# Input tiles scaled by ScalarE in the first layer, and VectorE's late weights in pieces over more steps

## The chip, the cores and the metric

The kernel runs on one core of a Trainium2 chip. The metric is the device time of one execution in microseconds; for the kernel before, the median of three runs is 833.73 (832.03 to 834.83). Engines are named TensorE (PE in the rows), VectorE (DVE), ScalarE (ACT), GpSimd (POOL) and SyncE (SP).

## The reference

The input x is 8 sequences of 512 rows by 128 columns. Four blocks follow, each as `x = x + layernorm(block(layernorm(x)))`:

```
block 1: 6 layers of   x = softmax(q) @ (softmax(k)^T v) @ wo + bo + x      (8 heads, on layernorm(x))
                       x = leaky_relu(layernorm(x) @ w1) @ w2 + x
block 2: squared relu of x @ W_fc^T, @ W_proj^T, then 5 steps of a spiking unit, counted
block 3: x @ Win^T + bin; k = sum_n C*dB*exp(logdA*t); a convolution by rfft/irfft of length 1024;
         + u * Dp; @ Wout^T + bout
block 4: token shift, sigmoid gate and squared relu key, value
```

The first `layernorm(x)` of block 1 is what part one of the change computes elsewhere: `(x - m) / sqrt(v + eps)` for each sequence. The spectrum of k, which depends on weights alone, is what part two spreads out.

## The kernel before, in words

**Layout.** X holds the whole input (8 x 512 columns), XI the running stream. A sequence is 4 tiles of 128x128. An item is one sequence in one layer: 48 items, item n is sequence b = n % 8 of layer n // 8. Every engine has a function `step(n, b, layer)` that lists, in the order in which this engine executes them, operations of item n and of earlier items (`run(f, n - 2)` is f for item n-2). `layers(step)` unrolls steps 0 to 43; what follows is an order written out by hand. Engines wait for each other by counting semaphores alone, so a step of one engine may be early or late against another's.

**One item.** ScalarE makes XR (L929), XI times a root RSTD that GpSimd computed. TensorE turns it (L317; its start is the beginning of a step on TensorE), ScalarE copies it out twice (XTH, XTF, L934), VectorE takes the difference XTL (L1363). TensorE makes keys and queries. VectorE takes the keys' maximum NKM (L1379), ScalarE the exponential EK (`keys_exp`, L976) and the copy QF, VectorE turns QF into QB (L1389) and takes the maximum QMX (L1395), GpSimd subtracts it (`queries_shift`, L772), ScalarE takes the exponential (L998), VectorE sums (L1399) and inverts (L1405), GpSimd multiplies (`queries_scale`, L777), VectorE turns it to QS (L1356). ScalarE's XR of the next item (L929) stands behind the queries' exponential. Two steps later the second half of the item: X2H and X2F from ScalarE, X2L from VectorE (`second_low`, L1329), then four hidden blocks on TensorE (X2H, X2L with W1) and their products with W2.

**The first layer's input.** For each sequence VectorE computes mean and variance (`input_stats`, L1264 and L1267, to STX and MVX), GpSimd the root of the variance (`input_rstd`, L721 to L727, to RX and VNX), and then XI = (X - mean) * RX. For sequence 0 this last is VectorE's, for the other seven it is GpSimd's `input_norm` (L731): four tiles of 128x128 with two columns of scalars each. It stands at the end of GpSimd's step n for sequence n+3, ahead of `join(n + 1)`, which joins the statistics of the stream (JOIN, L743 to L749), `first_root` (RSTD, L767) and `queries_shift`.

**The weights of later blocks.** In steps 31 to 41 the spectrum of block 3's kernel is made beside the layers. CENTRE is step 33, CENTRE_IN step 34. VectorE's `late_weights(n)` adds Dp to KTM in step 33, makes sums and differences of KTM in steps 34 to 36 (`butterfly_pairs`, `butterfly_even`, `butterfly_odd`, to FLY and KV), and in step 34 also NMU and the centred WOUTT and BOUT (L1425 to L1429). It stands in VectorE's step between `first_stats` and `second_low`:

```
                run(first_stats, n + 2)
...
                late_weights(n)
...
                run(second_low, n - 2)
                run(masked, n)
```

KTM is complete at the end of step 32 (`k_out`), KV is needed in step 37 (`ktm`), the centred weights by the last blocks (`mixed`). `part_done` makes an engine wait for its own instruction before it goes on. `keep_busy` on TensorE multiplies CE1 into a bank that is not used yet, to fill steps 0 to 2.

## Time and profile before

| | before |
|---|---|
| median of 3 runs | 833.73 us (832.03 to 834.83) |
| the profiled execution, its own time | 833.7 us |
| its span | 831.3 us |
| TensorE busy | 771.9 us, 93% |
| VectorE busy | 663.1 us, 80% |
| ScalarE busy | 579.2 us, 70% |
| GpSimd busy | 442.4 us, 53% |

The profile describes one execution. The span runs from the first to the last instruction; the execution's own time is 2.4 us longer. A busy share is an average over the whole span, so it doesn't say which engine sets the pace of a stretch. For that one reads what ended an engine's idle time (in square brackets behind an instruction), and the granted clock of TensorE.

### The profile page before, as it was taken

The numbers are of one execution on the slowest core, as the hardware profiler recorded it, in microseconds if no ns is written. First come the engines' busy times: TensorE is split into PE (matmuls) and PEld (weight loads), VectorE is DVE, ScalarE is ACT, GpSimd is POOL, SyncE is SP. The second block draws the span as 40 slices with busy tenths as digits, with TensorE's granted clock in tenths as the row PEclk, the third lists the DMA queues.
The fourth block names the chain that finished last, engine by engine and source line by source line (L and its number), as shares of the span: only waits on it lengthen the run. The fifth ranks groups of instructions, "written<-read, shape, count | busy, mean of one in ns | idle before, by whom it ended". The sixth has DMA issues, their size and how long they took to land.

```text
span 831.3 us, 16083 instructions
## 1 busy us (share of the span) xinstructions
PE 771.9 (93%) x5266; PEld 674.8 (81%) x5274; DVE 663.1 (80%) x1957; ACT 579.2 (70%) x1252; POOL 442.4 (53%) x724
## 2 busy tenths in 40 slices
PE   7689999999999999999999999999999999997672
PEld 3478889999999999999988898988878977885651
DVE  4667888788777887778787777788868999999873
ACT  3476777787777777777875777768885586755464
POOL 6888455555466544544452443644554244555454
PEclk9999999999999999999999999999999999999988
DMA  9300000100010000100001000000000000000001
GB/s 252 106 1 1 1 1 2 39 2 1 1 39 2 1 2 1 40 2 1 1 2 39 1 1 1 2 1 1 2 1 1 2 0 2 2 13 0 27 13 52
DMA packets 19728, 13.69 MB, mean 16 GB/s; under 512 B 2488, under 2 KB 18495, under 8 KB 19647
## 3 DMA queue, kind: packets, MB, share of 16 engines
q1 hardware_dynamic: 19646, 12.67, 5.4%
q8 instruction: 43, 0.70, 0.4%
q14 instruction: 39, 0.31, 0.1%
HBM read 10.57 MB, written 2.10 MB: 15 GB/s over the span
## 4 chain that ended last, share of the span: by engine, by line
PE 72%; DVE 13%; POOL 8%; issue 4%; ACT 2%; DMA 0%; POOLq 0%; DVEq 0%; ACTq 0%
PE PS L307 65%; PE PS L317 7%; POOL XI L731 3%; DVE ST L1196 2%; POOL RX L722 1%; DVE MV L1199 1%; POOL QB L772 1%; DVE BIG L1503 1%; POOL RSTD L767 1%; ACT XI L886 1%; POOL R L689 1%; DVE STX L1264 0%; DVE BIG L1552 0%; DVE BIG L1496 0%; DVE BIG L1497 0%
## 5 line engine op out<-in xcount | busy, mean ns | idle before, releaser
L307 PE MATMUL PS<-W,HL 128*128 128x128 f32 x1536 | 202.6, 275 | 0.0
L307 PEld LDWEIGHTS PS<-W,HL 128*128 128x128 f32 x1536 | 194.1, 192 | 9.8 <-issue 1.4
L942 ACT ACTIVATE HL<-PS 128x512 f32<-128x512 f32 x192 | 109.9, 596 | 17.7 <-PE PS L307 13.9
L743 POOL TENSOR_TENSOR JOIN<-STATS 128x8 f32<-128x8 f32 (+1 forms) x48 | 12.0, 249 | 184.5 <-DVE STATS L1279 184.5
L307 PE MATMUL PS<-X2H,W1L 128*128 128x512 f32 x192 | 89.1, 464 | 3.3 <-issue 3.0
L976 ACT ACTIVATE EK<-PS,NKM 128x512 f32<-128x512 f32 x48 | 33.1, 689 | 75.4 <-DVE NKM L1379 75.4
L777 POOL TENSOR_TENSOR QB<-QB,QRC 128x512 f32<-128x512 f32 x48 | 50.9, 1060 | 55.7 <-DVE QRC L1405 55.7
L307 PE MATMUL PS<-X2H,W1H 128*128 128x512 f32 x192 | 76.4, 398 | 0.0
L307 PE MATMUL PS<-X2L,W1H 128*128 128x512 f32 x192 | 76.1, 396 | 0.0
L1279 DVE BATCH_NORM_STATS2 STATS<-XI 128x6 f32<-128x128 f32 x352 | 75.5, 278 | 0.1
L317 PE MATMUL PS<-ID,XR 128*128 128x128 f32 x384 | 59.0, 276 | 8.6 <-ACT XR L929 8.6
L934 ACT ACTIVATE XTH<-PS,LNC,SC 128x512 fp32r<-128x512 f32 x48 | 37.4, 779 | 42.1 <-PE PS L317 42.1
L689 POOL TENSOR_TENSOR R<-VE,MHALF 128x4 f32<-128x4 f32 x56 | 61.0, 1089 | 4.7
L929 ACT ACTIVATE XR<-XI,RSTD 128x128 f32<-128x128 f32 x192 | 61.0, 394 | 3.4 <-POOL RSTD L767 3.4
L688 POOL TENSOR_SCALAR VE<-MV 128x4 f32<-128x4 f32 x56 | 13.4, 240 | 90.6 <-DVE MV L1199 88.4
L760 POOL TENSOR_TENSOR RSTD<-JOIN,MHALF 128x4 f32<-128x4 f32 x48 | 61.0, 1271 | 0.2
L317 PEld LDWEIGHTS PS<-ID,XR 128*128 128x128 f32 x384 | 46.4, 146 | 15.0 <-issue 12.1
L307 PE MATMUL PS<-MM,QS 128*128 128x128 f32 x384 | 53.7, 284 | 1.8 <-DVE QS L1356 1.8
L307 PE MATMUL PS<-EKT,XR 128*128 128x128 f32 x384 | 51.0, 276 | 1.6 <-ACT EKT L881 1.6
L772 POOL TENSOR_TENSOR QB<-QB,QMX 128x512 f32<-128x512 f32 x48 | 51.9, 1081 | 0.2 <-DVE QMX L1395 0.2
L1389 DVE STREAM_TRANSPOSE QB<-QF 128x512 f32<-128x512 f32 x48 | 34.1, 711 | 22.4 <-ACT QF L881 21.9
L307 PEld LDWEIGHTS PS<-MM,QS 128*128 128x128 f32 x384 | 47.5, 195 | 4.4 <-issue 4.3
(217 smaller groups left out, 2091.9 us busy)
## 6 DMA issues: line engine op xcount, KB each, us to landing
W<-in_w SPq DMA_DIRECT2D x12, 256.0 KB
X<-in_x SPq DMA_DIRECT2D x8, 256.0 KB, 4.6
out<-X SPq DMA_DIRECT2D x8, 256.0 KB, 2.3
QKV<-in_qkv SPq DMA_DIRECT2D x6, 192.0 KB, 2.7
FWD<-in_fwd SPq DMA_DIRECT2D x1, 1024.0 KB, 5.4
INV<-in_inv SPq DMA_DIRECT2D x1, 1024.0 KB, 8.1
WO<-in_wo SPq DMA_DIRECT2D x6, 64.0 KB
FWDX<-in_fwdx SPq DMA_DIRECT2D x1, 256.0 KB, 5.7
```

The lines of the kernel that those rows point to most:

```text
L307: return nc.tensor.matmul(o, l, r, start=start, stop=stop, skip_group_check=True)
L317: last = nc.tensor.transpose(o[:, j * P:(j + 1) * P], i[:, j * P:(j + 1) * P], ID[:, :])
L689: return pool.tensor_tensor(RS[k][:, :], VES[k][:, :], MHALF[:, 0:TILES], ALU.pow)
L760: pool.tensor_tensor(RSTD[:, TILES:2 * TILES], JOIN[:, 4, TILES:2 * TILES], MHALF[:, TILES:2 * TILES], ALU.pow).then_inc(s["ln2_rstd"], 1)
L772: pool.tensor_tensor(heads(QB[:, :]), heads(QB[:, :]), QMX[:, :].unsqueeze(2).broadcast_to([P, 32, DH]), ALU.subtract).then_inc(s["q_sub"], 1)
L777: pool.tensor_tensor(heads(QB[:, :]), heads(QB[:, :]), QRC[:, :].unsqueeze(2).broadcast_to([P, 32, DH]), ALU.mult).then_inc(s["q_nrm"], 1)
L929: last = nc.scalar.activation(o[:, j * P:(j + 1) * P], tile(src, b, j), ACT.Copy, scale=r[:, first + j:first + j + 1])
L934: return nc.scalar.activation(o[:, :], i[:, :], ACT.Identity, scale=SC[slot][:, which:which + 1], bias=LNC[slot][:, 2 * which + 1:2 * whic ...
L942: nc.scalar.activation(HL[f][:, :], pH[f % 2][:, :], ACT.Prelu, alpha=LEAK).then_inc(s["hl"], 1)
L976: nc.scalar.activation(EK[:, :], pK[:, :], ACT.Exp, bias=NKM[:, 0:1], accum_out=KSM[:, 0:1]).then_inc(s["ek"], 1)
L1279: last = nc.vector.bn_stats(STATS[:, first + j, :], tile(src, b, j))
L1389: nc.vector.transpose(QB[:, :], QF[:, :]).then_inc(s["q_blk"], 1)
```

## The change

Part one: GpSimd's `input_norm` becomes `input_mean`, which computes -mean * RX for the four tiles in two 128x4 operations, to NMX. ScalarE gets `input_norm`: XI = X * RX + NMX, one activation with scale and bias columns per tile (`normalise`, L886 before). It stands ahead of `keys_exp` in steps 0 (sequence 1) and 1 to 5 (sequences 3 to 7), and behind `weights_copy` in step 0 (sequence 2). VectorE's `input_stats(n + 3)` moves from the end of the step to the place behind `first_stats`. Sequence 0 stays on VectorE.

Part two: of `late_weights`, NMU and WOUTT go to step 27 (MIXED = 3 * 8 + 3), BOUT to step 28, both behind `second_stats`. The butterfly is split: `band_sums` behind `second_stats`, ahead of the queries' blocks, and `band_differences` behind `second_low`, each in the same steps as before.

```diff
+MIXED = 3 * BATCH + 3
...
-            def input_norm(b):
-                for j in range(b * TILES, (b + 1) * TILES):
-                    last = pool.tensor_scalar(XI[:, j * P:(j + 1) * P], X[:, j * P:(j + 1) * P], MVX[:, 2 * j:2 * j + 1],
-                                              RX[:, j:j + 1], ALU.subtract, ALU.mult)
-                last.then_inc(s["xi_init"], 1)
+            def input_mean(b):
+
+                cols = slice(b * TILES, (b + 1) * TILES)
+                mean = MVX[:, b * 2 * TILES:(b + 1) * 2 * TILES].rearrange("p (j t) -> p j t", t=2)[:, :, 0]
+                part_done(pool.tensor_tensor(NMX[:, cols], mean, RX[:, cols], ALU.mult))
+                pool.tensor_scalar(NMX[:, cols], NMX[:, cols], -1.0, 0.0, ALU.mult, ALU.add).then_inc(s["i_nm"], 1)
...
                     input_rstd(n + 3)
-                    input_norm(n + 3)
+                    input_mean(n + 3)
...
+            def input_norm(b):
+                act.wait_ge(s["i_nm"], b)
+                tiled = slice(b * TILES, (b + 1) * TILES)
+                normalise(seq(XI, b), seq(X, b), RX[:, tiled], NMX[:, tiled]).then_inc(s["xi_init"], 1)
...
                 run(rectified, n - 3, 2)
+                if n == 0:
+                    input_norm(1)
+                if 1 <= n < BATCH - 2:
+                    input_norm(n + 2)
                 run(keys_exp, n)
...
                 run(weights_copy, n)
+                if n == 0:
+                    input_norm(2)
...
+            def band_sums(n):
+                if n == CENTRE:
+                    dve.wait_ge(s["k_out"], 2)
+                    part_done(tt(KTM[0:1, 0:P], KTM[0:1, 0:P], DP[0:1, :], ALU.add))
+                if n == CENTRE + 1:
+                    tt(FLY[:, 0:2 * P], KTM[:, 0:2 * P], KTM[:, 2 * P:4 * P], ALU.add)
+                if n == CENTRE + 2:
+                    ts(FLY[:, 4 * P:6 * P].rearrange("p (i c) -> p i c", c=P),
+                       FLY[:, 0:4 * P].rearrange("p (i h c) -> p i h c", i=2, h=2)[:, :, 1], 0.5 ** 0.5, None, ALU.mult)
+                    tt(KV[:, 0:P], FLY[:, 0:P], FLY[:, P:2 * P], ALU.add)
+                if n == CENTRE + 3:
+                    tt(tile(KV, 0, 2), KTM[:, 0:P], FLY[:, 5 * P:6 * P], ALU.add)
+                    tt(tile(KV, 0, 3), FLY[:, 4 * P:5 * P], KTM[:, 2 * P:3 * P], ALU.add)
...
+            def band_differences(n):
+                if n == CENTRE + 1:
+                    part_done(tt(FLY[:, 2 * P:4 * P], KTM[:, 0:2 * P], KTM[:, 2 * P:4 * P], ALU.subtract))
+                if n == CENTRE + 2:
+                    tt(KV[:, P:2 * P], FLY[:, 0:P], FLY[:, P:2 * P], ALU.subtract)
+                    part_done(nc.vector.tensor_copy(KV[:, 4 * P:6 * P], FLY[:, 2 * P:4 * P]))
+                if n == CENTRE + 3:
+                    tt(tile(KV, 0, 6), KTM[:, 0:P], FLY[:, 5 * P:6 * P], ALU.subtract)
+                    tt(tile(KV, 0, 7), FLY[:, 4 * P:5 * P], KTM[:, 2 * P:3 * P], ALU.subtract).then_inc(s["ktm"], 1)
...
                 run(second_stats, n - 1)
+                late_weights(n)
+                band_sums(n)
...
                 run(first_stats, n + 2)
+                if n + 3 < BATCH:
+                    input_stats(n + 3)
...
-                late_weights(n)
...
                 run(second_low, n - 2)
+                band_differences(n)
                 run(masked, n)
                 run(queries_sum, n)
                 run(queries_reciprocal, n)
                 run(second_residual, n - 3)
-                if n + 3 < BATCH:
-                    input_stats(n + 3)
```

How the orders stand. ScalarE from the second copy of the turned stream to the exponential of the keys in step 3, before and then in the change (HL are hidden blocks, EK the keys' exponential):

```order
L934 ACTIVATE XTF<-PS,LNC,SC 128x512
L942 ACTIVATE HL<-PS 128x512 x2
L976 ACTIVATE EK,KSM<-PS,NKM 128x512
L881 ACTIVATE QF<-PS 128x512
L942 ACTIVATE HL<-PS 128x512
```

```order
L936 ACTIVATE XTF<-PS,LNC,SC 128x512
L949 ACTIVATE HL<-PS 128x512 x2
L888 ACTIVATE XI<-X,NMX,RX 128x128 x4
L983 ACTIVATE EK,KSM<-PS,NKM 128x512
L883 ACTIVATE QF<-PS 128x512
L949 ACTIVATE HL<-PS 128x512
```

Four tiles of XI now stand directly ahead of EK.

VectorE in step 2, from the queries' maximum to the end of the step, before and then in the change:

```order
L1395 TENSOR_REDUCE QMX<-QB 128x32
L1383 RECIPROCAL KRC<-KSM 128x1
L1329 TENSOR_TENSOR X2L<-X2F,X2H 128x512
L1411 TENSOR_TENSOR CT<-PS,HMASK 128x128
L1399 TENSOR_REDUCE QSM<-QB 128x32
L1405 RECIPROCAL QRC<-QSM 128x32
L1264 BN_STATS STX<-X 128x6 x4
L1267 BN_AGGR MVX<-STX 128x2 x4
```

```order
L1408 TENSOR_REDUCE QMX<-QB 128x32
L1396 RECIPROCAL KRC<-KSM 128x1
L1277 BN_STATS STX<-X 128x6 x4
L1280 BN_AGGR MVX<-STX 128x2 x4
L1342 TENSOR_TENSOR X2L<-X2F,X2H 128x512
L1424 TENSOR_TENSOR CT<-PS,HMASK 128x128
L1412 TENSOR_REDUCE QSM<-QB 128x32
L1418 RECIPROCAL QRC<-QSM 128x32
```

The statistics of X have moved ahead of X2L.

VectorE in step 34, from the stream's statistics to the mask, before and then in the change:

```order
L1279 BN_STATS STATS<-XI 128x6 x4
L1292 TENSOR_TENSOR FLY<-KTM 128x256
L1293 TENSOR_TENSOR FLY<-KTM 128x256
L1425 TENSOR_SCALAR NMU<-MU 128x2
L1427 BN_STATS WST<-WOUTT 128x6
L1428 BN_AGGR WMV<-WST 128x2
L1429 TENSOR_SCALAR WOUTT<-WOUTT,WMV 128x128
L1427 BN_STATS WST<-BOUT 128x6
L1428 BN_AGGR WMV<-WST 128x2
L1429 TENSOR_SCALAR BOUT<-BOUT,WMV 128x128
L1329 TENSOR_TENSOR X2L<-X2F,X2H 128x512
L1411 TENSOR_TENSOR CT<-PS,HMASK 128x128
```

```order
L1292 BN_STATS STATS<-XI 128x6 x4
L1431 TENSOR_TENSOR FLY<-KTM 128x256
L1402 STREAM_TRANSPOSE QB<-QF 128x512
L1408 TENSOR_REDUCE QMX<-QB 128x32
L1396 RECIPROCAL KRC<-KSM 128x1
L1292 BN_STATS STATS<-XI 128x6 x4
L1342 TENSOR_TENSOR X2L<-X2F,X2H 128x512
L1442 TENSOR_TENSOR FLY<-KTM 128x256
L1424 TENSOR_TENSOR CT<-PS,HMASK 128x128
```

X2L follows the statistics at once, one FLY stands ahead of QB and one behind X2L. TensorE's and SyncE's orders are the same in both kernels.

## Rows read from the trace of the kernel before

**Rows 1.** The page, part 1: busy time, share of the span, instructions of each engine.

```profile
PE 771.9 (93%) x5266; PEld 674.8 (81%) x5274; DVE 663.1 (80%) x1957; ACT 579.2 (70%) x1252; POOL 442.4 (53%) x724
```

**Rows 2.** The chain of waits over 0 to 120 us, shares by line.

```profile
by line: PE PS L307 23.4%; POOL XI L731 18.5%; POOL RX L722 6.8%; POOL QB L772 6.0%; issue 5.5%; POOL RSTD L767 5.1%; PE PS L317 3.4%; DVE STX L1264 3.3%; POOL VNX L725 2.7%; DMA X<-in_x 2.3%; DVE QSM L1399 1.7%; POOL QB L777 1.7%; ACT QB L
```

**Rows 3.** Stretches from turn to turn: length; busy of PE, PEld, DVE, ACT, POOL; clock, DMA, GB/s.

```profile
24.37:36.33 11.96, 8.46 (x37) 5.53 (x37) 8.17 (x25) 5.40 (x13) 11.12 (x19) 0.86 0.25 72
36.33:48.61 12.28, 8.88 (x46) 6.02 (x47) 8.87 (x26) 6.78 (x15) 11.36 (x21) 1.00 0.01 2
...
61.30:74.32 13.02, 12.02 (x82) 10.43 (x83) 9.38 (x27) 8.78 (x19) 10.71 (x19) 1.00 0.00 0
74.32:87.33 13.01, 12.02 (x82) 10.43 (x83) 9.99 (x31) 8.78 (x19) 10.69 (x19) 1.00 0.01 2
526.92:538.43 11.51, 11.51 (x83) 10.40 (x82) 9.02 (x23) 8.67 (x18) 6.54 (x11) 1.00 0.00 1
```

**Rows 4.** Timeline of step 4: start, duration, engine, line, operation [idle before it <- what ended it].

```profile
61.17 1.06 POOL L777 TENSOR_TENSOR QB<-QB,QRC 128x512 f32<-128x512 f32 x1 [0.88 <-DVE QRC L1405]
...
62.92 0.20 POOL L721 TENSOR_SCALAR VEX<-MVX 128x4 f32<-128x4 f32 x1 [0.69 <-DVE MVX L1267]
...
65.58 3.13 POOL L731 TENSOR_SCALAR XI<-X,MVX,RX 128x128 f32<-128x128 f32 x4
...
66.70 0.69 ACT L976 ACTIVATE EK<-PS,NKM 128x512 f32<-128x512 f32 x1 [2.32 <-DVE NKM L1379]
...
68.95 0.69 DVE L1395 TENSOR_REDUCE QMX<-QB 128x32 f32<-128x512 f32 x1
...
70.73 0.69 DVE L1329 TENSOR_TENSOR X2L<-X2F,X2H 128x512 fp32r<-128x512 f32 x1 [1.02 <-ACT X2F L934]
...
70.95 1.39 POOL L772 TENSOR_TENSOR QB<-QB,QMX 128x512 f32<-128x512 f32 x1
...
74.58 0.86 DVE L1264 BATCH_NORM_STATS2 STX<-X 128x6 f32<-128x128 f32 x4
...
75.47 0.38 DVE L1267 BATCH_NORM_AGGREGATE MVX<-STX 128x2 f32<-128x6 f32 x4
```

**Rows 5.** Timeline of step 0's end: the mask, its matmul, and the turn of step 1.

```profile
18.40 0.27 DVE L1233 TENSOR_SCALAR MBV<-HMASK,BIAS 128x128 f32<-128x128 f32 x1
...
19.29 0.38 PE L307 MATMUL PS<-WO,MBV 128*128 128x128 f32 x2
...
24.37 0.63 PE L317 MATMUL PS<-ID,XR 128*128 128x128 f32 x4 [2.92 <-ACT XR L929]
```

**Rows 6.** Timeline of step 34.

```profile
431.04 0.71 DVE L1389 STREAM_TRANSPOSE QB<-QF 128x512 f32<-128x512 f32 x1 [0.75 <-ACT QF L881]
...
432.92 0.78 ACT L934 ACTIVATE X2F<-PS,LNC,SC 128x512 f32<-128x512 f32 x1
...
433.65 1.18 POOL L760 TENSOR_TENSOR RSTD<-JOIN,MHALF 128x4 f32<-128x4 f32 x1
433.89 0.41 DVE L1293 TENSOR_TENSOR FLY<-KTM 128x256 f32<-128x256 f32 x1
...
436.14 0.68 DVE L1329 TENSOR_TENSOR X2L<-X2F,X2H 128x512 fp32r<-128x512 f32 x1
...
436.92 0.47 PE L307 MATMUL PS<-X2H,W1L 128*128 128x512 f32 x1 [1.85 <-issue]
```

**Rows 7.** Stretches of steps 34, 35 and 36, columns as in rows 3.

```profile
424.82:439.12 14.30, 12.45 (x85) 11.11 (x84) 12.20 (x33) 9.07 (x19) 7.38 (x12) 0.96 0.01 2
439.12:452.16 13.04, 12.62 (x84) 11.41 (x83) 9.95 (x26) 8.78 (x18) 4.57 (x10) 0.91 0.23 61
452.16:464.11 11.95, 11.65 (x83) 10.56 (x82) 10.06 (x27) 8.79 (x18) 5.09 (x10) 1.00 0.01 2
```

**Rows 8.** ScalarE's timeline: the same form of activation on X, in a later block.

```profile
683.89 1.64 ACT L886 ACTIVATE XI<-X,NM,R 128x128 f32<-128x128 f32 x4
```

**Rows 9.** Waits of the whole span: engine and line, what it waited for, us, times, longest.

```profile
DVE CT L1411 <- PE PS L307: 31.8, 41, 2.0
```

More of the change, by code:

```diff
@@ L183, in build @@
         STX, MVX = sb("STX", [BATCH * TILES * 6]), sb("MVX", [BATCH * TILES * 2])
-        VEX, RX, VNX = (sb(n, [BATCH * TILES]) for n in ("VEX", "RX", "VNX"))
+        VEX, RX, VNX, NMX = (sb(n, [BATCH * TILES]) for n in ("VEX", "RX", "VNX", "NMX"))
         XR2 = sb("XR2", [SEQ])
@@ L226, in build @@
             "bias_out bias_ps bm_out bm_ps bo_c c_in c_ps ce1 ce1_zero ct e1 e1_arg e2 e2_arg eighth ek ekT_ps "
-            "ek_tm fc_out fc_ps g_ps gt h_ps hl i_rstd i_var k_fm k_out k_ps k_rec kf kf_ps kmax ktm la la_exp "
+            "ek_tm fc_out fc_ps g_ps gt h_ps hl i_nm i_rstd i_var k_fm k_out k_ps k_rec kf kf_ps kmax ktm la la_exp "
             "late_in ln1_rstd ln2_rstd ln_part m_ps m_ready mbv mixed out_ps p_part q0_in q_blk q_exp q_fm "
@@ L854, in _ @@
             input_rstd(1)
-            input_norm(1)
+            input_mean(1)
             input_rstd(2)
-            input_norm(2)
+            input_mean(2)
             layers(step)
@@ L1411, in masked @@
                 tt(CT[:, :], pK[:, P:2 * P], HMASK[:, :], ALU.mult).then_inc(s["ct"], 1)
-            def late_weights(n):
+            def band_sums(n):
                 if n == CENTRE:
@@ L1417, in late_weights @@
                 if n == CENTRE + 1:
-                    butterfly_pairs(KTM)
+                    tt(FLY[:, 0:2 * P], KTM[:, 0:2 * P], KTM[:, 2 * P:4 * P], ALU.add)
                 if n == CENTRE + 2:
-                    butterfly_even(KV)
+                    ts(FLY[:, 4 * P:6 * P].rearrange("p (i c) -> p i c", c=P),
+                       FLY[:, 0:4 * P].rearrange("p (i h c) -> p i h c", i=2, h=2)[:, :, 1], 0.5 ** 0.5, None, ALU.mult)
+                    tt(KV[:, 0:P], FLY[:, 0:P], FLY[:, P:2 * P], ALU.add)
                 if n == CENTRE + 3:
-                    butterfly_odd(KTM, KV).then_inc(s["ktm"], 1)
-                if n == CENTRE_IN:
+                    tt(tile(KV, 0, 2), KTM[:, 0:P], FLY[:, 5 * P:6 * P], ALU.add)
[9 more added lines that the diff above has]
+                    tt(tile(KV, 0, 7), FLY[:, 4 * P:5 * P], KTM[:, 2 * P:3 * P], ALU.subtract).then_inc(s["ktm"], 1)
+            def late_weights(n):
+                if n == MIXED:
                     dve.wait_ge(s["late_in"], LATE_LOADS)
                     ts(NMU[:, :], MU[:, :], -1.0, 1.0, ALU.mult, ALU.add)
-                    for t in (WOUTT, BOUT):
-                        part_done(nc.vector.bn_stats(WST[:, :], t[:, :]))
+                for at, weights in ((MIXED, WOUTT), (MIXED + 1, BOUT)):
+                    if n == at:
+                        part_done(nc.vector.bn_stats(WST[:, :], weights[:, :]))
                         part_done(nc.vector.bn_aggr(WMV[:, :], WST[:, :]))
-                        last = ts(t[:, :], t[:, :], WMV[:, 0:1], None, ALU.subtract)
+                        last = ts(weights[:, :], weights[:, :], WMV[:, 0:1], None, ALU.subtract)
+                if n == MIXED + 1:
                     last.then_inc(s["mixed"], 1)
```

## The prediction

> **What bounds the kernel now.** The page comes first: TensorE is busy 93% of the span [rows 1], the others 53 to 80%, so a gain must be time in which TensorE waits or runs below full speed. There are two such places that the change touches. I call the start of a step on TensorE its turn (the first transpose of XR); step n works on item n.
>
> First place, steps 0 to 6. The chain of waits over the first 120 us names GpSimd's input tiles (L731) for 18.5%, more than any other line but the matmuls [rows 2]. The table of stretches, cut at the turns 24.37, 36.33, 48.61, 61.30, 74.32 and 87.33, shows what that does [rows 3]: steps 4 and 5 take 13.02 and 13.01 us for 82 matmul records, while a step of the same work late in the stack (83 records, TensorE never idle) takes 11.51. So 11.51 is the floor of a full step; steps 3 to 5 (12.69, 13.02, 13.01) stand 4.2 us above it together. Steps 1 and 2 hold only 37 and 46 records and run at the latency of one item's chain. In step 4 this chain can be read [rows 4]: GpSimd scales the queries (to 62.23), computes the next sequence's rstd, writes its tiles for 3.13 us, joins the statistics, and so reaches the queries' shift (L772) at 70.95, though the maximum it needs was there at 69.64. Step 0 ends with 2.92 us in which TensorE waits for XR [rows 5].
>
> Second place, steps 34 to 36. VectorE's spectrum pieces and the last weights stand ahead of X2L. X2F is ready at 433.70, X2L starts at 436.14, TensorE stands still for 1.85 us and goes on at 436.92 [rows 6]. Behind that the granted clock falls from 2.4 to 1.2 GHz for a while: it is 0.96 and 0.91 of full speed on average over steps 34 and 35 [rows 7].
>
> Between them and from there to the last layers TensorE is full, and the order of every engine is fixed, so what is won in either place moves everything behind it by the same amount.
>
> **The change, part 1: the input tiles.** GpSimd loses 7 times 3.13 us and gets two 128x4 operations instead, each as VEX's 0.20 [rows 4], 0.55 us with their issue: it is freed of 7 x 2.58, about 18 us, all in the first 85. ScalarE gets 7 times four activations that read a scale and a bias column from memory. The nearest row is the same form on X much later: four take 1.64 us [rows 8]. VectorE keeps its work, but input_stats, 0.86 + 0.38 = 1.27 us with the gap [rows 4], moves from the end of a step to the place ahead of X2L, and in step 0 ahead of the mask that TensorE's output bias waits for. Step by step, until the turns agree with the floor:
>
> - Step 0. With the tiles on ScalarE (in its waits for the keys' maximum and the transposed weights) XR is ready at about 21 by the same durations, and TensorE comes to the turn when its own merge is done, 24.37 - 2.92 = 21.45. The moved statistics push the mask by 1.27; it was ready at 18.67 and used at 19.29, so of the 0.62 of slack I count 0.42 as usable. The turn comes at about 22.3: gain 2.92 - 0.85 = 2.1 [rows 5].
> - Steps 1 and 2. The new tiles of item n+2 stand ahead of keys_exp on ScalarE, wait there for GpSimd's mean, and take 1.64. By step 4 (below) the exponential comes 0.5 us late; here the keys are not held up by other matmuls, so I estimate 1. Everything of the item is queued behind it, and in step 2 the moved statistics (1.27) also stand ahead of X2L. Against this stand GpSimd's lateness at the shift, 70.95 - 69.64 = 1.3 in step 4, and the slow clock of step 1 (0.86 on average [rows 3]), which I expect gone with the 2.92 us wait ahead of it. I take step 1 as 0.15 and step 2 as 0.6 slower, an estimate: turns at 34.4 and 47.3, gain 1.3 so far.
> - Steps 3 and 4. The mean is ready 0.93 (end of L777) + 3.35 - 0.69 (the chain to the tiles, less the idle before it, for which the moved statistics come earlier) + 0.55 = 4.2 us after the turn; the tiles end at 5.8, the exponential starts at 5.9 instead of 5.40. The maximum of the queries is 0.5 later, the statistics' 1.27 follow, and X2L starts at 10.1 instead of 9.43. This is 0.7 over the floor: 12.2 instead of 12.69 and 13.02, gain 0.5 and 0.8.
> - Step 5 has no statistics left; the shift follows the maximum at once (8.9 instead of 9.65), XR is ready before TensorE is, and the step costs 11.7 instead of 13.01: gain 1.3. Step 6 has no tile in either kernel and its own VectorE work (decay): unchanged.
>
> Sum of part 1: 1.3 + 0.5 + 0.8 + 1.3 = 3.9 us. The bounds: at best steps 3 to 5 sit on the floor and step 0 gains its whole 2.92, together 7.1; at worst the steps gain nothing and steps 1 and 2 each lose a whole 1.64 against step 0's 2.1, that is -1.2. What hides the tiles is ScalarE's idle time before the exponential, 2.32 us in step 4; without it each group would cost its 1.64.
>
> **Part 2: the spectrum.** In step 34 nine VectorE instructions leave the place ahead of X2L. One FLY addition goes behind second_stats, into a wait of 0.75 us for QF [rows 6], one subtraction behind X2L, where VectorE waits for TensorE ahead of CT (31.8 us in 41 waits [rows 9]), and the rest to steps 27 and 28 into the same wait. X2L then starts with X2F, at 433.7, over a microsecond before TensorE asks for it. What returns, with step 36 as the measure (11.95 us, TensorE busy 11.65 of them [rows 7]): in step 34 the idle 1.85 and, for the slow clock, 12.45 - 11.65 - 0.25 for one matmul more = 0.55; in step 35 the idle 13.04 - 12.62 = 0.42 and the slow clock's 12.62 - 11.65 = 0.97; in step 36 the idle 0.30, ahead of which the same pieces stand. Together 4.1. The bounds are 0 and 4.1 plus a few tenths. The seven other instructions took 436.14 - 434.30 = 1.84, so steps 27 and 28 get some 0.9 each in a wait of 0.75 and may come 0.3 late; step 33's KTM addition shares its wait with W2M and may make the queries 0.4 late. I cost these at 0, because X2L still waits for X2F behind them; without that cover they cost 0.3 + 0.3 + 0.4 = 1.0. No DMA moves, and no order on TensorE or SyncE.
>
> One row and one rule differ. The FLY subtraction, with two inputs in SBUF, ran from 433.89 to 434.30 inside GpSimd's pow of 433.65 to 434.83 [rows 6]; nothing blocked it. By the Trainium skill, "SBUF — State Buffer", section "SBUF: two separate sides", a VectorE instruction with two SBUF inputs and a GpSimd instruction share a port pair as an exclusive lock, and the later one waits for the whole of the earlier one. By that rule the pieces behind X2L in steps 34 to 36 would wait for GpSimd's pow, 3 x 0.4 us, and the time would be 826.9; the trace speaks against it here, for a pow of 4 columns at least.
>
> **Sum.** 3.9 + 4.1 = 8.0 less. The profiled execution took 833.7 (span 831.3), the median of the three runs is 833.73, so both give 825.7.
>
> **The rivals.**
> - A, full first layer: the late exponential is absorbed, since the keys are not what TensorE wants next, and part 1 gives step 0's 2.1 and the 4.2 to the floor, 6.3. For it: ScalarE had 2.32 us of idle there. Against it: X2L stands behind QMX and the moved statistics. 833.7 - 10.4 = 823.3.
> - B, poor first layer: the tiles ahead of the exponential take back what GpSimd gives, or the clock falls once more in the thin steps 1 to 3 (TensorE is busy 8.5 to 8.9 of their 12 us [rows 3]). With 1.5 lost in steps 1 and 2 each and 1.6 gained in steps 3 to 5, part 1 gives 2.1 - 3.0 + 1.6 = 0.7: 828.9.
> - C, part 2 stays short: something else is late for X2L in step 34, or the pieces behind X2L wait for GpSimd's pow. TensorE idles 1 us and the clock may fall again: part 2 gives 1 to 2.8: 828.8 to 827.0. The row of the free overlap and X2F at 433.70 speak against it.
> - D, slower: the tiles on ScalarE become the bound of steps 1 to 5. Each step is longer by 1.64, 8.2 in all, and TensorE's longer waits let the clock fall twice at the 1.5 that it cost in steps 34 and 35: 8.2 + 3.0 - 2.1 - 4.1 = 5.0 slower, 838.7. It decides from the point at which GpSimd's mean comes later than the keys' maximum plus the slack of the shift (0.85 us); I have it 0.5 too late.
> - The change doing something else than it says: the listing of the orders excludes that.
>
> **How the numbers follow.** Forecast 0.60, A 0.17, B 0.12, C 0.06, D 0.03, and 0.02 for both parts weak at once. Predicted: 825.7. The range 822.5 to 829.5 takes in A with a microsecond to spare, and B and C. A measurement of this kernel can tell about 0.3%, 2.5 us: faster means below 831.2. All but D and the doubly weak case and a slice of B lie there: faster 0.93, same 0.04, slower 0.03.
>
> **What would show it.** In the profile after: no granted clock below 1.00 from 430 to 450, no idle on TensorE ahead of X2H,W1L in steps 34 to 36 and X2L following X2F at once; turns at about 22, 34, 47, 59.5, 71.8 and 83.5; the four tiles on ScalarE at 1.64 us, directly ahead of the exponential, which starts 5.8 to 6 us after the turn. The step that I trust least is the price of that order in steps 1 to 4. If the exponential starts as early as before, A is right; if steps 3 and 4 stay at 13, B. If a clock of 0.5 remains near step 34, my reading of part 2 is wrong.

## The result, and the profile after

The median of four runs went from 833.45 us to 823.40 (822.92 to 823.64); the ratio is 0.9868, 95% interval 0.9841 to 0.9894. That is 10.05 us less, where 8.0 had been forecast. Measured once more later, beside the experiments, the change had a median of 825.49 over five runs against 833.83 (ratio 0.9899, 0.9874 to 0.9924), 8.3 less. Both medians lie in the forecast range; the forecast 825.7 is 2.3 above the first and 0.2 above the second. Why the change itself moves between 822.9 and 827.7 is a question of its own below. One of the six executions of part 1 alone took 1119.06 us at a mean clock of 0.651; its median below is that of the other five.

The profiled execution took 823.64 us with a span of 821.6, against 833.7 and 831.3. Busy times are those of the page, part 1; the columns are as in [rows 1].

```profile
PE 768.5 (94%) x5274; PEld 672.3 (82%) x5274; DVE 661.7 (81%) x1957; ACT 588.0 (72%) x1280; POOL 424.8 (52%) x710
```

GpSimd has 17.6 us less, ScalarE 8.8 more. The chain of waits over the first 120 us, by line, answers to [rows 2]:

```profile
by line: PE PS L308 39.9%; PE PS L318 7.5%; ACT XI L888 6.7%; POOL RX L723 5.1%; issue 4.8%; POOL QB L779 4.4%; ACT EK L983 3.6%; DMA X<-in_x 2.4%; POOL VNX L726 2.3%; DVE QSM L1412 2.0%; DVE STX L1277 1.4%; DVE QRC L1418 1.2%; DVE QB L1402
```

GpSimd's tiles are gone from it, ScalarE's have 6.7% in place of 18.5%, and the matmuls' share has risen from 23.4 to 39.9%. The stretches from turn to turn, steps 0 to 5, columns as in [rows 3]:

```profile
9.89:22.04 12.15, 8.40 (x39) 5.31 (x40) 6.78 (x29) 9.20 (x23) 6.41 (x15) 1.00 1.04 305
22.04:33.88 11.84, 6.98 (x39) 4.51 (x37) 8.79 (x27) 6.91 (x16) 8.23 (x17) 1.00 0.48 137
33.88:46.84 12.96, 9.84 (x46) 7.25 (x47) 8.79 (x25) 8.73 (x19) 9.25 (x20) 0.87 0.01 2
46.84:58.76 11.92, 11.71 (x84) 10.45 (x83) 8.80 (x25) 9.99 (x22) 7.53 (x17) 1.00 0.00 0
58.76:70.70 11.94, 11.73 (x83) 10.44 (x82) 9.27 (x27) 9.99 (x22) 7.55 (x17) 1.00 0.01 1
70.70:82.61 11.91, 11.70 (x84) 10.33 (x83) 8.95 (x23) 9.96 (x22) 7.97 (x17) 1.00 0.01 2
```

Steps 3 to 5 now take 11.9 us, 0.4 over the floor (11.51); step 0 is 2.5 shorter (the turn before it was at 9.72, now at 9.89); step 2 is longer than before and at 0.87 of full clock. Step 4 in the timeline, which answers to [rows 4]:

```profile
59.77 0.19 POOL L722 TENSOR_SCALAR VEX<-MVX 128x4 f32<-128x4 f32 x1
...
62.82 1.65 ACT L888 ACTIVATE XI<-X,NMX,RX 128x128 f32<-128x128 f32 x4 [1.00 <-POOL NMX L735]
...
64.38 0.67 ACT L983 ACTIVATE EK<-PS,NKM 128x512 f32<-128x512 f32 x1
...
65.04 0.58 ACT L883 ACTIVATE QF<-PS 128x512 f32<-128x512 f32 x1
...
65.19 0.66 PE L318 MATMUL PS<-ID,EK 128*128 128x128 f32 x4 [0.21 <-ACT EK L983]
...
66.39 0.69 DVE L1408 TENSOR_REDUCE QMX<-QB 128x32 f32<-128x512 f32 x1
...
67.06 0.85 DVE L1277 BATCH_NORM_STATS2 STX<-X 128x6 f32<-128x128 f32 x4
67.16 1.06 POOL L774 TENSOR_TENSOR QB<-QB,QMX 128x512 f32<-128x512 f32 x1 [0.62 <-DVE QMX L1408]
...
68.25 0.66 DVE L1342 TENSOR_TENSOR X2L<-X2F,X2H 128x512 fp32r<-128x512 f32 x1
```

Counted from the turn at 58.76, the exponential starts at 5.62 (before: 5.40), because the keys' maximum is there at 4.65 (before: 5.37) and the tiles hold it up by 0.97. QF starts at 6.28 (6.27), QMX at 7.63 (7.65), GpSimd's shift at 8.40 (9.65) and X2L at 9.49 (9.43). The exponential is 0.2 late and TensorE waits 0.21 for it; nothing behind it is late. X2F is ready at 9.16 and X2L starts 0.33 behind it, where the statistics end.

Step 34, which answers to [rows 6]:

```profile
428.39 0.78 ACT L936 ACTIVATE X2F<-PS,LNC,SC 128x512 f32<-128x512 f32 x1
...
429.20 0.69 DVE L1342 TENSOR_TENSOR X2L<-X2F,X2H 128x512 fp32r<-128x512 f32 x1 [0.42 <-ACT X2F L936]
429.21 1.54 POOL L762 TENSOR_TENSOR RSTD<-JOIN,MHALF 128x4 f32<-128x4 f32 x1
429.81 0.42 DVE L1442 TENSOR_TENSOR FLY<-KTM 128x256 f32<-128x256 f32 x1
```

X2L starts 0.03 us behind X2F's end, and TensorE has no idle time there. The stretches of steps 34, 35 and 36, against [rows 7]:

```profile
420.28:432.08 11.80, 11.80 (x86) 10.68 (x85) 9.67 (x25) 8.94 (x19) 6.82 (x12) 1.00 0.01 1
432.08:443.69 11.61, 11.61 (x83) 10.40 (x82) 9.96 (x27) 8.65 (x18) 5.67 (x10) 1.00 0.24 69
443.69:455.22 11.53, 11.53 (x84) 10.41 (x83) 9.98 (x27) 8.66 (x18) 5.67 (x10) 1.00 0.01 2
```

From turn to turn the whole difference of the two profiled executions can be written down: turn 7 comes 4.70 earlier (99.46 to 94.76); from there to turn 33 the change takes 0.17 more; turn 33 to turn 37 takes 47.31 instead of 51.67, 4.36 less; turns 37 to 47 take the same (129.31); behind turn 47 it is 237.08 instead of 237.91, 0.83 less; and 0.36 less outside the span. 4.70 - 0.17 + 4.36 + 0.83 + 0.36 = 10.08, within rounding the 10.06 between the two times.

### The profile page after: what moved, and what is told of

Its sections match the earlier page's. It is cut to its first block, busy times and chain, and to the rows that moved or that the text cites. A ratio compares the mean times of both kernels' runs of the same rounds, so it can differ in the third digit from the quotient of the medians.

```text
span 821.6 us, 16107 instructions
## 1 busy us (share of the span) xinstructions
PE 768.5 (94%) x5274; PEld 672.3 (82%) x5274; DVE 661.7 (81%) x1957; ACT 588.0 (72%) x1280; POOL 424.8 (52%) x710
## 4 chain that ended last, share of the span: by engine, by line
PE 75%; DVE 13%; POOL 4%; ACT 3%; issue 3%; DMA 0%; POOLq 0%; DVEq 0%; ACTq 0%
PE PS L308 67%; PE PS L318 8%; DVE ST L1209 2%; ACT XI L888 2%; DVE BIG L1533 1%; DVE MV L1212 1%; POOL RX L723 1%; POOL QB L779 1%; POOL R L690 1%; ACT EK L983 1%; DVE BIG L1582 0%; DVE BIG L1526 0%; DVE BIG L1527 0%; DVE QSM L1412 0%; DVE BIG L1556 0%
## 5 line engine op out<-in xcount | busy, mean ns | idle before, releaser
L949 ACT ACTIVATE HL<-PS 128x512 f32<-128x512 f32 x192 | 109.6, 595 | 14.8 <-PE PS L308 11.3
L745 POOL TENSOR_TENSOR JOIN<-STATS 128x8 f32<-128x8 f32 (+1 forms) x48 | 12.5, 260 | 189.3 <-DVE STATS L1292 189.3
L308 PEld LDWEIGHTS PS<-EKT,XR 128*128 128x128 f32 x384 | 47.6, 195 | 3.3 <-ACT EKT L883 2.3
```

What stands on the lines that cost most here:

```text
L308: return nc.tensor.matmul(o, l, r, start=start, stop=stop, skip_group_check=True)
L949: nc.scalar.activation(HL[f][:, :], pH[f % 2][:, :], ACT.Prelu, alpha=LEAK).then_inc(s["hl"], 1)
```

## The experiments

Twelve runs were made in three sets, each on a chip of its own, where the kernel before had medians of 834.75, 835.41 and 833.83. So medians of different sets are compared by their ratios: in this table a ratio is to the kernel before in the same set; the other columns are of the profiled execution: the periods of steps 0 to 5 between turns, the stretch from turn 33 to turn 37, and what lies behind turn 47 (us).

| kernel | median | ratio (95%) | steps 0 to 5 | 33 to 37 | tail |
|---|---|---|---|---|---|
| before | 833.45 | 1 | 14.6 12.0 12.3 12.7 13.0 13.0 | 51.67 | 237.9 |
| change | 823.40 | 0.9868 (0.9841 to 0.9894) | 12.1 11.8 13.0 11.9 11.9 11.9 | 47.31 | 237.1 |
| change, again | 825.49 | 0.9899 (0.9874 to 0.9924) | 13.2 12.5 13.1 11.7 12.0 11.9 | 47.33 | 237.2 |
| part 1 alone | 828.63 | 0.9918 (0.9888 to 0.9949) | 12.2 12.5 12.5 12.0 12.0 11.9 | 51.83 | 237.7 |
| part 2 alone | 830.16 | 0.9949 (0.9929 to 0.9969) | 14.7 12.5 12.3 12.7 13.0 13.0 | 47.29 | 239.0 |
| change, statistics late | 825.89 | 0.9886 (0.9852 to 0.9919) | 11.6 12.5 12.4 12.3 12.7 12.7 | 47.30 | 239.1 |
| before, statistics early | 832.78 | 0.9974 (0.9953 to 0.9995) | 14.6 12.0 12.5 12.7 12.4 12.3 | 50.17 | 238.3 |
| mean first | 822.95 | 0.9863 (0.9829 to 0.9897) | 12.2 11.3 11.6 11.9 11.5 11.5 | 47.29 | 237.4 |
| tiles behind context | 826.51 | 0.9905 (0.9868 to 0.9942) | 12.1 12.2 12.4 12.6 12.6 12.6 | 47.30 | 238.3 |
| filled | 825.34 | 0.9888 (0.9859 to 0.9917) | 12.2 11.9 12.3 11.9 12.0 11.9 | 47.33 | 237.9 |
| weights back | 826.88 | 0.9910 (0.9879 to 0.9941) | 13.2 12.5 13.1 11.6 12.0 11.9 | 49.23 | 239.6 |
| butterfly back | 827.33 | 0.9923 (0.9899 to 0.9946) | 12.1 11.9 12.5 12.4 12.0 11.9 | 48.46 | 240.9 |
| mean first, filled | 822.55 | 0.9860 (0.9834 to 0.9885) | 12.2 11.3 12.2 11.9 11.5 11.5 | 47.34 | 238.2 |
| and third statistics late | 822.40 | 0.9857 (0.9831 to 0.9883) | 11.6 11.5 12.2 11.9 11.5 11.5 | 47.33 | 238.2 |

The theory at the start: the two parts act in their own stretches and add up; part 1 is GpSimd's time leaving the chain to the shift and XR; part 2 is the wait for X2L and its slow clock. The rivals: the tiles on ScalarE cost what GpSimd gave, or something else is late for X2L.

**Part 1 alone** (the change, with `late_weights` as before).

> Part one alone (tiles on ScalarE, means on GpSimd, input_stats moved; late weights as before). Theory: the two parts lie in different stretches and TensorE is full between them, so this saves what the turns of the first seven steps show, 4.7 us, give or take 0.5: about 828.7. Turn 7 at 94.8 as in the change; the idle 1.85 us and the clock fall near step 34 stay. Rival: the 0.9 us that the change saved behind step 47 belongs to part one's shift; then 827.8.

**Part 2 alone** (the kernel before, with `band_sums`, `band_differences` and the new `late_weights`).

> Part two alone (late weights and spectrum spread, input tiles on GpSimd as before). Theory: 4.1 us less, about 829.3; turn 7 at 99.5 as before; no clock below 1.00 near step 34. Rival: if the parts are not additive, the sum of the two savings differs from 10.1 by more than 1.

Part 1 alone changes steps 0 to 5 and leaves 33 to 37 at 51.83; its turn 7 is at 95.07 and its tail at 237.7, so the rival that gave it the change's shorter tail isn't borne out. Part 2 alone gives 47.29 and leaves the first steps, but for step 1, which runs at 0.79 of full clock instead of 0.86 and takes 12.5 instead of 12.0. Its turn 7 is 0.6 later than before's and its tail 1.1 longer. By its ratio it saves 4.3 us of that set's 834.75 (interval 2.6 to 5.9), where 4.1 was expected; part 1 alone saves 6.8 (4.3 to 9.3), where 4.7 was. The parts add up: the product of the two ratios is 0.9867, the change's own is 0.9868, and in the profiles their 4.39 and 4.38 us stand against the change's 4.70 and 4.36. From turn 7 to turn 33 no change absorbs them: this stretch takes 312.98 to 313.19 us in all fourteen profiles.

**Statistics late** and **statistics early**: the moved `input_stats` undone in the change, and done alone in the kernel before.

```diff
                 run(first_stats, n + 2)
-                if n + 3 < BATCH:
-                    input_stats(n + 3)
...
                 run(second_residual, n - 3)
+                if n + 3 < BATCH:
+                    input_stats(n + 3)
```

> The change with input_stats back at the end of VectorE's step. My forecast charged the moved statistics with 0.85 in step 0 and with 1.27 ahead of X2L in steps 2 to 4, against 0.69 for a later start of GpSimd's chain. If X2L sets the pace there, this is faster by up to 1.5 (822). If the mean's arrival ahead of the keys' exponential sets it, GpSimd's chain starts 0.69 later in each step, the exponential too, and this is slower by 0.5 to 2 (824 to 825.5), though step 0 gains some of its 0.85.

> The kernel before with input_stats moved and nothing else. If the place of the statistics alone pays (GpSimd's wait of 0.69 per step goes), it saves up to 0.69 in steps 2 to 5, about 2 us (831.5). If GpSimd's tiles are the whole bound, it changes less than 1 us either way, as step 0 loses nothing (TensorE waits 2.92 there anyway).

With the statistics late, step 0 is 0.58 shorter (11.56 for 12.14): that is what they cost ahead of the mask. But steps 3 to 5 are 1.9 longer together (12.31, 12.65, 12.65 for 11.91, 11.95, 11.90). So of the two expectations the second held, that undoing the move is slower (turn 7 is 1.3 later). In the kernel before, the move alone shortens steps 4 and 5 by 0.7 each; its ratio of 0.9974 also holds the 1.5 us by which 33 to 37 is shorter there, which no edit made (see below). I had booked the move as a cost only. What it gives stands in VectorE's timeline of the kernel before, at the start of step 4 (turn at 61.30):

```profile
61.55 0.86 DVE L1264 BATCH_NORM_STATS2 STX<-X 128x6 f32<-128x128 f32 x4
62.45 0.38 DVE L1267 BATCH_NORM_AGGREGATE MVX<-STX 128x2 f32<-128x6 f32 x4
62.74 0.32 DVE L1349 SCALAR_TENSOR_TENSOR MM<-PS,KRC,BM 128x128 f32<-128x128 f32 x1
62.98 0.70 DVE L1356 STREAM_TRANSPOSE QS<-QB 128x512 f32<-128x512 f32 x1
```

and in the change, there (turn at 58.76):

```profile
59.00 0.34 DVE L1362 SCALAR_TENSOR_TENSOR MM<-PS,KRC,BM 128x128 f32<-128x128 f32 x1
59.71 0.71 DVE L1369 STREAM_TRANSPOSE QS<-QB 128x512 f32<-128x512 f32 x1 [0.37 <-POOL QB L779]
```

At the end of a step the statistics stand ahead of the next step's MM and QS. QS starts 1.68 behind the turn before and 0.95 after; TensorE's MM,QS and the keys behind it, and so the keys' maximum, come 0.7 earlier. With the statistics late in the change, GpSimd waits for MVX again and the exponential comes at 6.37 (turn at 58.62):

```profile
60.28 0.19 POOL L722 TENSOR_SCALAR VEX<-MVX 128x4 f32<-128x4 f32 x1 [0.68 <-DVE MVX L1280]
...
63.44 1.65 ACT L888 ACTIVATE XI<-X,NMX,RX 128x128 f32<-128x128 f32 x4 [1.76 <-POOL NMX L735]
64.99 0.67 ACT L983 ACTIVATE EK<-PS,NKM 128x512 f32<-128x512 f32 x1
```

**Mean first.** -mean * RX is made ahead of VNX, which is needed later; `some(b)` is true for every sequence but the first.

```diff
                 pool.wait_ge(s["i_rstd"], b + 1)
+                if some(b):
+                    input_mean(b)
                 part_done(pool.tensor_tensor(VNX[:, cols], var, RX[:, cols], ALU.mult))
...
                     input_rstd(n + 3)
-                    input_mean(n + 3)
```

> The change with GpSimd's mean computed right behind the root, ahead of the three VNX operations: the mean is ready 1.0 to 1.3 us earlier. If the tiles ahead of the keys' exponential set the pace (the change's steps 3 to 5 stand at 11.92, 11.94 and 11.91 against the floor of 11.51, with 0.21 idle ahead of the turned exponential), each of these steps comes to 11.5 to 11.6 and step 2 loses a part of its 1.73 idle: turn 7 about 2 us earlier, at 92.7 to 93.2. If X2L or XR sets it, nothing moves (94.8).

**Tiles behind context.** `input_norm` behind `context_copy` in steps 1 to 5, in place of ahead of `keys_exp`.

> The change with ScalarE's tiles of steps 1 to 5 moved from ahead of the keys' exponential to behind the copy of the context, ahead of the queries' exponential. If the exponential's lateness costs the 0.4 per step, this gives it back: turn 7 at 93 to 93.5. If the tiles only move the lateness (XR of the next item stands right behind them, and ScalarE had under 1 us of idle there), XR is later by up to 1.6 a step and turn 7 comes at 95 to 98.

Step 4 of mean first (turn at 56.90):

```profile
60.16 1.65 ACT L887 ACTIVATE XI<-X,NMX,RX 128x128 f32<-128x128 f32 x4 [0.21 <-POOL NMX L737]
61.72 0.67 ACT L982 ACTIVATE EK<-PS,NKM 128x512 f32<-128x512 f32 x1
```

and of tiles behind context (turn at 59.02):

```profile
63.72 0.69 ACT L983 ACTIVATE EK<-PS,NKM 128x512 f32<-128x512 f32 x1 [1.61 <-DVE NKM L1392]
...
68.11 1.64 ACT L888 ACTIVATE XI<-X,NMX,RX 128x128 f32<-128x128 f32 x4
69.65 0.62 ACT L1005 ACTIVATE QB<-QB 128x512 f32<-128x512 f32 x1
70.17 1.27 ACT L931 ACTIVATE XR<-XI,RSTD 128x128 f32<-128x128 f32 x4
...
71.59 0.63 PE L318 MATMUL PS<-ID,XR 128*128 128x128 f32 x4 [0.94 <-ACT XR L931]
```

With the mean first the exponential starts at 4.82, TensorE doesn't wait for it, and steps 4 and 5 sit on the floor (11.51, 11.52). Turn 7 comes at 92.08, earlier than the expected 92.7 to 93.2: 0.5 is won in step 1, and 1.4 in step 2, where the change's profile had a slow clock. Step 3 stays at 11.88, since another wait takes the place of the first: GpSimd's product of W and W2M (44.29, 1.04 us) stands ahead of the scaling of the queries (45.29), and QS starts at 46.38, 1.36 behind the turn, where it starts 0.78 behind it in step 3 of the change. Behind context the exponential is early too (4.70), but the 1.64 us stand in front of XR, and TensorE waits 0.94 for XR: 12.57. Of the two places that were tried, the tiles are free only ahead of the exponential, and only if the mean comes first.

**Filled**: one piece of TensorE's filling work ahead of the turned weights.

```diff
+                if 1 <= n < 3:
+                    keep_busy(1)
                 run(weights_turn, n)
```

> The change with one more filling matmul on TensorE (0.86 us) in steps 1 and 2, in its wait for the keys' exponential (1.40 and 1.73 us idle in the change). In the change's profile the granted clock fell in step 2, behind these waits, and the matmuls on EKT took 1.95 instead of 1.16. If the idle time makes the clock fall, it stays at 1.00 here and step 2 takes 12.3 instead of 12.97 (turn 7 about 0.7 earlier). If not, nothing changes.

**Mean first and filled**; then also the third sequence's statistics at the end of VectorE's step 0; and **the change again**.

> The change with the mean ahead of VNX and with one piece of filling work on TensorE ahead of the turned weights in steps 1 and 2. If the mean shortens the chain to the exponential and the filling only prevents a clock fall (theory 1): turns as with the mean first alone (22.1, 33.4, 45.0, 56.9, 68.4, 79.9) within 0.3 us, clock 1.00 from 10 to 50, time 1.4 to 2.5 us below the change. If the filling delays what stands behind it by its own length (theory 2), the turns of steps 2 and 3 come 0.4 to 0.8 later.

> The kernel of e11 with the statistics of sequence 3 at the end of VectorE's step 0 instead of ahead of the mask. If these statistics hold the mask and with it the turn of step 1 (theory 1): step 0 takes 11.6 instead of 12.2 us. What step 1 makes of it is open: the mean of sequence 3 is made in step 0, so if it is still ahead of its use, step 1 stays at 11.3 and the time falls by 0.5; if the tiles of step 1 wait for it (theory 2), step 1 takes 0.5 to 1 more and nothing is won.

> The change itself once more, beside the others on this chip. If what a kernel takes behind turn 47 varies from execution to execution by the clock and not by the code: turns 1 to 7 at 22.04, 33.88, 46.84, 58.76, 70.70, 82.61, 94.76 within 0.4 us each unless the clock falls elsewhere, turn 33 to turn 37 at 47.3, and the tail anywhere from 237 to 239.6; time 823 to 826.

The change again answers where 2 us between two measurements of one kernel come from. Its turn 7 is at 96.35, 1.59 later than in the first profile, and its own time is 825.44, 1.80 more. Steps 0 to 2:

```profile
9.79:23.01 13.22, 9.79 (x38) 6.49 (x39) 7.25 (x30) 9.22 (x23) 6.42 (x15) 0.87 0.97 291
23.01:35.54 12.53, 8.32 (x39) 5.79 (x38) 8.29 (x26) 6.80 (x16) 8.48 (x17) 0.80 0.42 118
35.54:48.68 13.14, 10.65 (x47) 7.72 (x47) 9.43 (x27) 8.74 (x19) 9.28 (x19) 0.80 0.01 2
```

It starts behind the same waits in both. TensorE in step 0, the first profile and then this one:

```profile
15.41 0.66 PE L318 MATMUL PS<-ID,EK 128*128 128x128 f32 x4 [0.77 <-ACT EK L983]
16.75 1.16 PE L308 MATMUL PS<-EKT,XR 128*128 128x128 f32 x8 [0.69 <-ACT EKT L883]
```

```profile
15.30 0.66 PE L318 MATMUL PS<-ID,EK 128*128 128x128 f32 x4 [0.78 <-ACT EK L983]
16.64 1.87 PE L308 MATMUL PS<-EKT,XR 128*128 128x128 f32 x8 [0.69 <-ACT EKT L883]
```

Same code, same waits, 1.16 us and 1.87 for the same eight matmuls. The filling doesn't settle it either: filled had full clock in steps 1 and 2, but mean first and filled fell to 0.86 in step 2 although no wait for the exponential shows in steps 1 and 2 any more (the slow clock begins at 33.8, behind a wait of 0.91 us for XR), and mean first without filling stayed at full clock behind a wait of 0.98 for XR. Step 2 at full clock and below it: 12.33 (filled) against 12.96 (change), 11.59 (mean first) against 12.18 (mean first, filled). So a fall there is worth about 0.6 us, the filling costs little or nothing that can be measured, and it gives no protection that these runs show. What makes the clock fall in one execution and not in another stays open. Of the two theories on mean first and filled neither held as it stood: the turns are within 0.2 of mean first up to turn 2 and 0.4 later from there, and the clock fell in step 2. Of the third statistics theory 1 held: step 0 takes 11.56 instead of 12.15, step 1 11.45 instead of 11.34, turn 3 comes 0.36 earlier; the time, 822.40 against 822.55, can't show it.

**Weights back**: NMU, WOUTT and BOUT in step 34 as before, the butterfly split. **Butterfly back**: `butterfly_pairs`, `_even` and `_odd` whole in the old place, the weights in steps 27 and 28.

```diff
-MIXED = 3 * BATCH + 3
+MIXED = CENTRE_IN
...
-                late_weights(n)
                 band_sums(n)
...
+                late_weights(n)
```

```diff
-                band_sums(n)
...
+                if n == CENTRE + 1:
+                    butterfly_pairs(KTM)
...
                 run(second_low, n - 2)
-                band_differences(n)
```

> The change with NMU, WOUTT and BOUT back in step 34 at their old place, the butterfly still split. If those seven instructions are what held X2L (1.84 of the 2.4 us), X2L starts at about 1.4 us behind X2F, TensorE idles 0.8 to 1 us in step 34 and the clock may fall: 1 to 2.5 us slower than the change. The stretch from turn 33 to turn 37 takes 48.3 to 49.8 instead of 47.31. If the butterfly was what held it, the stretch stays at 47.3.

> The change with the sums and differences of steps 34 to 36 together again at their old place ahead of X2L, the seven instructions for the last weights still in steps 27 and 28. If those seven made the wait of step 34 (theory 1): turn 33 to turn 37 stays at 47.3 to 47.9 us, at most 0.4 us of idle on TensorE ahead of X2H,W1L per step, time within 0.6 us of the change. If the split butterfly matters as much (theory 2): each of the three steps loses its 0.4 to 0.8, 1.2 to 2.4 us together, turn 33 to turn 37 at 48.5 to 49.7.

Steps 34 to 36 of weights back, then of butterfly back:

```profile
421.87:435.62 13.75, 11.97 (x85) 10.75 (x84) 12.28 (x32) 9.06 (x19) 6.36 (x12) 1.00 0.01 1
435.62:447.21 11.59, 11.59 (x83) 10.40 (x82) 9.97 (x27) 8.66 (x18) 5.67 (x10) 1.00 0.24 69
447.21:458.72 11.51, 11.51 (x83) 10.40 (x82) 9.97 (x27) 8.67 (x18) 5.67 (x10) 1.00 0.01 2
```

```profile
420.19:432.22 12.03, 11.96 (x85) 10.83 (x84) 10.29 (x25) 9.06 (x19) 6.81 (x12) 1.00 0.00 1
432.22:444.32 12.10, 11.66 (x83) 10.56 (x82) 10.32 (x28) 8.78 (x18) 5.26 (x10) 1.00 0.24 66
444.32:456.27 11.95, 11.64 (x83) 10.56 (x82) 10.05 (x27) 8.79 (x18) 5.08 (x10) 1.00 0.01 2
```

Against the change's 47.31 the weights cost 1.92, all in step 34; the whole butterfly costs 1.15, all of it in steps 34 to 36 (0.23, 0.49 and 0.42). In weights back TensorE's wait was 1.78 us instead of the expected 0.8 to 1; one of the seven instructions (BOUT) took 1.14 us there instead of 0.29, which the last section comes back to. So for the butterfly the second theory was nearly right (1.2 to 2.4 expected), the first wrong: splitting it isn't worthless. 1.92 + 1.15 = 3.07 at full clock; before, early statistics alone had full clock in steps 34 to 36 too and took 50.17, 2.86 over 47.31. What is left to before's 51.67, 1.5 us, is the slow clock behind the 1.85 us wait [rows 6]. Part 1 alone had the same fall, behind a wait of 1.86. In weights back the wait was 1.78 us, with early statistics 1.85, and no fall followed. So this 1.5 us is lost in some executions and not in others.

The tail holds the same code in all these kernels and ran from 237.1 to 240.9 us. In the first 150 us behind turn 47 TensorE is busy for 146.3 to 146.8 us at full clock in every profile; the difference shows in the 70 us behind them. Of the change and of mean first and filled:

```profile
734.52:804.52 70.00, 48.89 (x302) 40.40 (x302) 61.78 (x218) 40.79 (x100) 37.76 (x64) 0.95 0.05 16
```

```profile
732.33:802.33 70.00, 51.83 (x302) 43.30 (x302) 60.84 (x218) 39.96 (x98) 37.15 (x62) 0.90 0.05 16
```

302 matmul records in both, at 0.95 and 0.90 of full clock; the tails are 237.1 and 238.2. Over all fourteen profiles the tail goes with the mean clock of these 70 us: 237.1 and 237.2 at 0.95, 237.4 to 237.9 at 0.93, 237.7 to 239.1 at 0.90, 239.6 and 240.9 at 0.88.

## Why the prediction came out as it did

The signs and the places held, and so did the mechanism of part 2. Part 1's gain was real, but two of its reasons were wrong, and the size of the whole was short by 2.1 us: 1.2 of that lie behind turn 47 and outside the span, where the sum had nothing. By its own steps, forecast gain and measured gain between the profiled executions:

| term | forecast | measured |
|---|---|---|
| step 0 | 2.1 | 2.5 |
| step 1 | -0.15 | 0.1 |
| step 2 | -0.6 | -0.7 |
| step 3 | 0.5 | 0.8 |
| step 4 | 0.8 | 1.1 |
| step 5 | 1.3 | 1.1 |
| part 2, steps 33 to 36 | 4.1 | 4.4 |
| behind turn 47 | 0 | 0.8 |
| outside the span | 0 | 0.4 |

The rest is 0.17 more for the start, 0.02 for step 6 and 0.17 for the stretch from turn 7 to turn 33.

**Step 0.** The statistics ahead of the mask were priced at 0.85 beyond their slack; they cost 0.58, as the two kernels without them show (11.56 us, where the sum had 14.64 - 2.92 = 11.72).

**Steps 3 and 4: the step that failed.** "The maximum of the queries is 0.5 later, the statistics' 1.27 follow, and X2L starts at 10.1 instead of 9.43." The tiles took 1.65 as forecast. X2L starts at 9.49, not at 10.1, and the step takes 11.9, not 12.2. I looked at the statistics only where they went, not at who stood behind them where they had been: MM and QS of the next step. With those 0.7 earlier the keys' maximum comes at 4.65 instead of 5.37, which pays for most of the 0.97 that the tiles add; the exponential starts at 5.62 (5.9 forecast), and QF and the queries' maximum are where they were. Nor are the statistics' 1.27 a cost ahead of X2L: VectorE had waited there for 1.02 us [rows 4], and X2L now starts 0.33 behind X2F and 0.06 later than before. Step 5, which has no statistics, takes the same 11.9 as steps 3 and 4, so they don't lengthen the step. I had added a cost to a row that had idle time before it. Undone, the move costs 1.9 us in steps 3 to 5. Of what is left over the floor in step 4, 0.4, the turned exponential brings 0.33 (it starts at 6.43, with mean first at 6.10) and the matmuls behind it 0.1; mean first removes both in steps 4 and 5.

**Step 2: the right number for the wrong reason.** I took 0.6 for the late exponential and for X2L. At full clock step 2 takes 12.33 (filled), as long as before (12.28), so against before the order costs nothing; the 0.6 is the granted clock, which fell behind waits of 1.40 and 1.73 us for the exponential. The sum had the slow clock as gone with the 2.92 us wait. In the first profile step 1 did run at full clock, but in five others with the tiles on ScalarE and without that wait it ran at 0.80 to 0.89. A clock fall in the thin steps was half of rival B: it came once in the first profile and three times in the change again.

**Part 2.** X2L behind X2F, no idle, clock 1.00: as forecast. The missing 0.3 is matmul time: steps 34 and 36 are busy for 11.80 and 11.53 where I had put 11.90 and 11.65. That 4.1 was partly a matter of luck is new: 1.5 of it is a clock fall that stood behind the wait of 1.85 us in two profiles (before, part 1 alone) and not in two others (statistics early, weights back).

**The tail: the other step that failed.** "Between them and from there to the last layers TensorE is full, and the order of every engine is fixed, so what is won in either place moves everything behind it by the same amount." Up to turn 47 this held within 0.2 us; behind it the sum had nothing, and 0.83 us came, with 0.36 outside the span. These 1.2 us of the 10.05 lie where no instruction was changed, and I count them as luck. The tail moves by more than that between kernels whose code there is the same, with the granted clock. The forecast's range should have taken that in: 237.1 to 240.9 at the tail of kernels with the same code there, and 1.6 us between two profiles of the change in steps 0 to 2.

**The rivals.** A (6.3 for part 1) didn't come with the change (4.9), and comes with mean first: turn 7 at 92.08, 7.4 us before the kernel before's. D needed GpSimd's mean to come later than the keys' maximum plus 0.85 us; in step 4 the maximum ends at 63.41 and the tiles had already begun at 62.82. C didn't show.

**The rule on the shared port.** I had said that nothing blocked the FLY subtraction inside GpSimd's root. That row holds, also after (0.42 at 429.81, inside the root from 429.21 to 430.75). The reading was too narrow: next to it, in the kernel before and in weights back, stand rows in which one engine does hold up the other; they are in the last section.

A version that beats the kernel before, and probably the change, is mean first, with or without the filling and the third statistics: 822.40 to 822.95. In one set the best of them took 822.40 and the change 825.49; but the intervals of their ratios, 0.9831 to 0.9883 and 0.9874 to 0.9924, just overlap, and the change's first ratio, 0.9868, is as good as theirs (0.9857 to 0.9863). So the times alone don't show the gain over the change; by the profiles it is 2.1 us at turn 7 with full clock in both (92.08 for mean first, 94.22 for filled).

## What to carry to other kernels

Of an instruction that moves, look at both places: at the idle time in front of whoever is queued behind it in the new one, and at who stood behind it in the old one: this move cost 0.6 us in step 0 and next to nothing in steps 3 to 5 where it went, and paid 1.9 where it came from. When work goes to an engine with idle time, put it where that idle time is and bring its operands forward first; the same four activations cost 0, 0.4 or 1.1 us a step by their place and by two small operations on GpSimd. And where the granted clock falls in one execution of a kernel and not in the next, compare turn by turn: medians of one kernel differed by 2 us, as much as taking the last weights out of step 34 was worth.
